# Keys and values on 64-row tiles in two parts, TensorE in groups of four chunks

## The chip, the cores and the metric

The kernel runs on one core of a Trainium2 chip. The metric is the device time of one launch in microseconds. Engines are named as in the profile: PE is TensorE's matmuls, PEld its weight loads, DVE is VectorE, ACT is ScalarE, POOL is GpSimd, SP is SyncE.

## The reference

A gated cross-attention block, followed by a mixture of experts. With LN for a layer norm without gain:

```
q = LN(x) Wq^T + bq            x: (32, 56, 256), 16 heads of 16
k, v = ctx Wk^T + bk, ctx Wv^T + bv      ctx: (32, 1500, 256)
p = softmax(clip(q k^T / 4, -50, 50))    masked keys at -50
d = clip(rs) * ((p v) Wo^T + bo)
x = x + tanh(g_xattn) * (LN(d) * gamma + beta)
router: top 2 of 8 experts on LN(x), softmax of the two logits
x = x + tanh(g_ffn) * sum_e w_e * relu(LN(x) Wfc_e)^2 Wproj_e
```

All is float32. The context has 48,000 rows of 256, so most of the work is keys and values, then scores and P times V.

## The kernel before

Float32 accuracy is reached with fp32r operands in two summands, high and low: a product is three matmuls (high x high, high x low, low x high). This holds for keys, values, scores and experts. P times V is a plain fp32 matmul, which the trace shows as two instructions.

**Tiling.** Batches are taken in pairs (`pair(i)`, 16 of them). The 1500 keys of a batch are 3 groups of 4 chunks of 125 keys, so a pair has 24 chunks (PC) in 6 groups (PG). `pair` runs over u = 0 to 11, two chunks each; q = u // 2 is the group and half = u % 2. While the chunks of group q are used, keys and values of the next group (n = i * PG + q + 1) are made, a half at each u.

**TensorE.** At each u: `scores` of two chunks, `k_proj` of one half (128 of the 256 key features for all 500 keys: 6 matmuls, 128 rows contracted, 500 columns), `v_proj` of one half (two chunks of keys, 12 matmuls, 128 rows contracted, 256 columns), on some u a side step (`spread_sums`, `x_transpose`, `q_proj`, `out_proj`, `y_transpose`, and the router in the last pair), then `pv` of the two chunks before. Scores use 64-row tiles, in pairs on rows 0-63 and 64-127. `pv` has 16 heads a chunk, on column tiles of 32.

**Buffers.** The scores have four banks of PSUM (`sc_ps`), two chunks. `k_ps` has a bank for each half; bank 0 is also the side steps' (`side_ps`). `v_ps` is one bank for both halves, and `o_ps` one. Keys (`kh`, `kl`), values (`vst`) and split context (`c_hi`, `c_lo`) are double in SBUF. The probabilities (`prob`) have PB = 4 buffers of one chunk.

**The other engines,** in an order written out by hand for each u. ScalarE: `ctx_high` (once a group), `exps` of two chunks, `k_hi_evac`, copies of the side steps. VectorE: `before_clips` (side work that depends on u), `ctx_low`, `clip` of two chunks, `k_lo_evac`, `v_evac_step`. GpSimd takes powers and some subtractions. SyncE loads a context group as soon as `ctx_low` has freed its buffer, and does the four `pack` DMAs behind the load of q = 0. Everything is ordered by semaphores: `pv` waits for `clip_done` and `v_evac`, `v_proj` for `v_evac` of the half before, `k_proj` for `k_lo`, `exps` for `scores_done` and for `pv_done` of the chunk PB earlier, `scores` for `exp_done` of the chunk two earlier.

After the attention the experts run over 7 tiles of 256 tokens. The change doesn't touch them but for the P times V that remains at their start.

Of the kernel before, what the change touches and what calls it, by code (L numbers as in the profile page):

```python
# [14 lines left out]
B, S, D, T = 32, 56, 256, 1500  # L15
NH, HD = 16, 16
P = 128
KD = D // P
TC = 125
GC = 4  # L20
# [14 lines left out]
FT = 256  # L35
NF = TOK // FT
VW = HD + 1
PB = 4
UN = PC // 2
NW = 2 * NE  # L40
NB = 4
# [12 lines left out]
def gated_cross_attention_moe(nc, a, x1_dram, out):  # L54
# [5 lines left out]
    with ExitStack() as ctx:  # L60
        def sem(name):
            return ctx.enter_context(nc.semaphore(name))
# [134 lines left out]
        ctx_split = sem("ctx_split")  # L197
        kproj_done = sem("kproj_done")
        vproj_done = sem("vproj_done")
        k_hi = sem("k_hi")  # L200
        k_lo = sem("k_lo")
        v_evac = sem("v_evac")
# [163 lines left out]
        def _(pe):  # L366
# [19 lines left out]
            def v_proj(n, half, s):  # L386
# [8 lines left out]
                                   wv_hi[:, k, :], wv_lo[:, k, :], k == 0, k == KD - 1)  # L395
                last.then_inc(vproj_done, 1)

            def scores(i, c):

                n = i * PC + c  # L400
                b, g = c // NC, c // GC
                if c % NC == 0:
                    pe.wait_ge(q_ready, 4 * i + 2 * b + 2)
                if c % GC == 0:
                    pe.wait_ge(k_lo, KD * (i * PG + g + 1))
                wait(pe, exp_done, n - 1)
                cs = slice(c % GC * TC, (c % GC + 1) * TC)
                for m in range(KD):
                    for term, (k, q) in enumerate(((kh, q_hi), (kh, q_lo), (kl, q_hi))):
                        for r in range(2):  # L410
                            rows = slice(r * HW, (r + 1) * HW)
                            last = pe.matmul(sc_ps[0:TC, 2 * (c % 2) + r, m * HS * S:(m + 1) * HS * S],  # L412
                                             k[rows, g % 2, m, cs], q[rows, b, m, :, :], start=term == 0, stop=term == 2)
                last.then_inc(scores_done, 1)

            def pv(i, c):

                n = i * PC + c
                if c % NC == 0:
                    wait(pe, o_evac, 2 * i + c // NC)  # L420
                if c % 2 == 0:
                    pe.wait_ge(v_evac, i * UN + c // 2 + 1)
# [52 lines left out]
            def pair(i, first=False, final=False):  # L475
                freed = {}
                if not first:
                    freed.update({0: (ylo_done, i), 2: (sum_evac, i), 8: (dlt_evac, i)})
                if not final:
                    freed.update({4: (xT_done, i + 2), 6: (qT_done, i + 2)})  # L480
                for u in range(UN):
                    q, half = divmod(u, 2)
                    n = i * PG + q + 1
                    more = not (final and q == PG - 1)
                    scores(i, 2 * u)
                    if first and u == 0:
                        pe.wait_ge(v_evac, 2)
                    scores(i, 2 * u + 1)
                    if more:
                        k_proj(n, half, (q + 1) % 2, freed.get(u))  # L490
                        v_proj(n, half, (q + 1) % 2)
                        if half == 1:
                            pe.wait_ge(k_lo, KD * n + 1)
                    if u == 1 and not first:
                        spread_sums(i - 1)
                    if u == 3 and not final:
                        x_transpose(i + 1)
                    if u == 5 and not final:
                        q_proj(i + 1)
                    if u == 7 and not first:  # L500
                        out_proj(i - 1)
                    if u == 10 and final:
# [5 lines left out]
                    if u == 11 and not first:  # L508
                        y_transpose(i - 1)
                    if first and u == 1:  # L510
                        pe.wait_ge(o_clear, 1)
                    if not (first and u == 0):
                        for d in (2, 1):
                            pv(*((i, 2 * u - d) if u > 0 else (i - 1, PC - d)))

            pe.wait_ge(cst_in, 16)
            x_transpose(0, first_side)
# [59 lines left out]
            pe.wait_ge(welo_done, NW)  # L577
            pe.wait_ge(exp_done, B * NC - 1)
            fc(0, 0)
            for d in (2, 1):  # L580
                pv(NP - 1, PC - d)
            experts(0, first=True)
            experts(1)
# [7 lines left out]
        def _(act):  # L591
# [65 lines left out]
            def pair(i, first=False, final=False):  # L657
                for u in range(UN):
                    q, half = divmod(u, 2)
                    if u == 0 and not final:  # L660
                        load_xq(i + 1)
                    if u == 10:
                        if not first:
                            store_x1(i - 1)
                        load_xr(i)
                        if not final:
                            load_matrix(i + 1)
                    if half == 0 and not (final and q >= PG - 2):
# [5 lines left out]
                    if u == 1:  # L674
                        if not first:
                            sums_spread(i - 1)
                        expert_hi(i)
                    if u == 3 and not final:
                        x_transposed(i + 1)
                    if u == 11 and not first:  # L680
                        y_transposed(i - 1)
                    if u == 11 and final:
                        second_of_two(0)

# [52 lines left out]
        def _(dve):  # L737
# [179 lines left out]
            def pair(i, first=False, final=False):  # L917
                for u in range(UN):
                    q, half = divmod(u, 2)
                    before_clips(i, u, first, final)  # L920
                    if not (final and q >= PG - 2):
                        ctx_low(i * PG + q + 2, half, q % 2)
                    clip(i, 2 * u)
                    clip(i, 2 * u + 1)
                    if not (final and q == PG - 1):
                        k_lo_evac(i * PG + q + 1, half, (q + 1) % 2)
                        v_evac_step(i * PG + q + 1, half, (q + 1) % 2)
                if not first:
                    y_low(i - 1)

            def before_clips(i, u, first, final):

                if u == 0:
                    q_split(i, 1)
                if u == 1:
                    if not first:
                        o_evac_step(i - 1, 1)
                        sums_split(i - 1, 1)
                    q_high(i, 1)
                if u == 2:  # L940
                    if not final:
# [15 lines left out]
                if u == 6 and not final:  # L957
                    q_evac(i + 1)
                    q_split(i + 1, 0)
                if u == 7:  # L960
                    o_evac_step(i, 0)
                    sums_split(i, 0)
                    if not final:
                        q_high(i + 1, 0)
                if u == 8:
                    if not first:
                        delta(i - 1)
# [168 lines left out]
```

## Time and profile before

| | us |
|---|---|
| median of 3 runs | 1268.37 (1267.36 to 1270.18) |
| profiled execution, its own time | 1267.26 |
| its span | 1265.1 |
| mean granted TensorE clock | 0.997 |
| busy: PE, PEld, DVE, ACT, POOL | 1248.7, 1129.9, 964.8, 688.5, 174.6 |

The span reaches from the first to the last instruction; the time is 2.2 us longer. Matmuls are pipelined: the duration of one (0.28 us, say) is longer than the time to the start of the next, so pitches are read from starts.

### The profile page before, as it was taken

What the parts mean: (1) busy time and instruction counts of PE and PEld (TensorE: products, weight loads), DVE (VectorE), ACT (ScalarE), POOL (GpSimd) and SP (SyncE); (2) the same over time, 40 slices, a digit from 0 to 9 for tenths busy, and PEclk for the clock granted to TensorE, in tenths of its full rate; (3) what the DMA queues carried; (4) which work ended last, traced back from release to release, by engine and by line L of the source; (5) the groups of instructions that cost most, each with busy time, mean ns of one, the idle gap of its engine ahead of it and who ended that gap; (6) DMA issues with size and microseconds to landing.
All of it is one profiled execution on the core that took longest, in us unless ns stands there. A gap on an engine that the chain in (4) does not pass through costs nothing.

```text
span 1265.1 us, 51469 instructions
## 1 busy us (share of the span) xinstructions
PE 1248.7 (99%) x22040; PEld 1129.9 (89%) x22040; DVE 964.8 (76%) x1806; ACT 688.5 (54%) x854; POOL 174.6 (14%) x142
## 2 busy tenths in 40 slices
PE   7999999999999999999999999999999999899998
PEld 6888888888888888888888888888888888899998
DVE  6678777878787877787777878787878777687555
ACT  5555555556555556565555555565555565344443
POOL 1000101010101010010001010101010100154443
PEclk9999999999999999999999999999999999899999
DMA  5121212121112112121211121211121120010000
GB/s 158 52 67 43 64 53 70 53 66 56 55 51 68 55 42 71 47 70 53 70 50 57 53 70 53 67 55 54 51 69 55 45 74 5 19 64 10 17 8 17
DMA packets 29507, 68.19 MB, mean 54 GB/s; under 512 B 6037, under 2 KB 13458, under 8 KB 29330
## 3 DMA queue, kind: packets, MB, share of 16 engines
q1 hardware_dynamic: 20450, 54.61, 14.2%
q10 hardware_dynamic: 8880, 10.75, 2.6%
q8 instruction: 168, 2.75, 0.9%
q14 instruction: 9, 0.07, 0.0%
HBM read 60.77 MB, written 3.67 MB: 51 GB/s over the span
## 4 chain that ended last, share of the span: by engine, by line
PE 94%; issue 2%; DVE 1%; POOL 1%; ACT 0%; DMA 0%; DVEq 0%; POOLq 0%; ACTq 0%
PE sc_ps L412 23%; PE o_ps L427 14%; PE k_ps L369 10%; PE v_ps L370 7%; PE v_ps L369 7%; PE v_ps L371 7%; PE k_ps L371 7%; PE k_ps L370 7%; PE sc_ps L369 3%; PE sc_ps L370 3%; PE sc_ps L371 3%; PE k_ps L444 1%; POOL h_lo L352 1%; PE k_ps L457 1%; DVE h_sq L1043 0%
## 5 line engine op out<-in xcount | busy, mean ns | idle before, releaser
L610 ACT ACTIVATE prob<-sc_ps,m_bias 125x896 f32<-125x896 f32 x384 | 366.3, 1005 | 321.8 <-PE sc_ps L412 321.8
L915 DVE TENSOR_SCALAR prob<-prob 125x896 f32<-125x896 f32 x384 | 245.1, 642 | 140.8 <-ACT prob L610 137.4
L412 PE MATMUL sc_ps<-q_hi,kh 64*125 64x224 f32 x1536 | 228.5, 294 | 0.0
L370 PE MATMUL v_ps<-wv_lo,c_hi 128*125 128x256 f32 x764 | 214.8, 281 | 0.0
L369 PE MATMUL v_ps<-wv_hi,c_hi 128*125 128x256 f32 x764 | 214.3, 280 | 0.0
L371 PE MATMUL v_ps<-wv_hi,c_lo 128*125 128x256 f32 x764 | 214.0, 280 | 0.0
L412 PE MATMUL sc_ps<-q_hi,kl 64*125 64x224 f32 x1536 | 209.8, 270 | 0.0
L412 PE MATMUL sc_ps<-q_lo,kh 64*125 64x224 f32 x1536 | 209.3, 269 | 0.0
L427 PE MATMUL o_ps<-prob,vst 125*17 125x56 f32 x12288 | 189.2, 214 | 0.0
L427 PEld LDWEIGHTS o_ps<-prob,vst 125*17 125x17 f32 x12288 | 158.3, 98 | 31.5 <-issue 9.8
L763 DVE SCALAR_TENSOR_TENSOR kl<-k_ps,cst,kh 128x500 fp32r<-128x500 f32 x192 | 141.5, 738 | 46.5 <-ACT kh L597 44.7
L369 PE MATMUL k_ps<-c_hi,wk_hi 128*128 128x500 f32 x384 | 169.7, 442 | 0.9 <-DVE c_lo L769 0.9
L412 PEld LDWEIGHTS sc_ps<-q_hi,kh 64*125 64x125 f32 x1536 | 144.8, 185 | 17.7 <-issue 0.2
L597 ACT ACTIVATE kh<-k_ps,cst 128x500 fp32r<-128x500 f32 x192 | 130.5, 680 | 43.3 <-PE k_ps L371 41.0
L371 PE MATMUL k_ps<-c_hi,wk_lo 128*128 128x500 f32 x384 | 149.6, 390 | 0.0
L370 PE MATMUL k_ps<-c_lo,wk_hi 128*128 128x500 f32 x384 | 149.3, 389 | 0.0
L370 PEld LDWEIGHTS v_ps<-wv_lo,c_hi 128*125 128x125 f32 x764 | 141.8, 186 | 7.6
L369 PEld LDWEIGHTS v_ps<-wv_hi,c_hi 128*125 128x125 f32 x764 | 141.9, 186 | 7.2
L316 POOL TENSOR_TENSOR rstd<-var_e,mhalf 112x1 f32<-112x1 f32 x48 | 69.2, 1442 | 560.1 <-DVE var_e L753 560.1
L412 PEld LDWEIGHTS sc_ps<-q_hi,kl 64*125 64x125 f32 x1536 | 145.9, 187 | 0.0
L412 PEld LDWEIGHTS sc_ps<-q_lo,kh 64*125 64x125 f32 x1536 | 145.4, 186 | 0.0
L371 PEld LDWEIGHTS v_ps<-wv_hi,c_lo 128*125 128x125 f32 x764 | 141.9, 186 | 0.0
(129 smaller groups left out, 1913.7 us busy)
## 6 DMA issues: line engine op xcount, KB each, us to landing
raw<-in_ctxT SPq DMA_DIRECT2D x96, 500.0 KB, 3.5
w_raw<-in_we ACTq DMA_DIRECT2D x16, 256.0 KB, 3.7
xq<-in_x ACTq DMA_DIRECT2D x16, 112.0 KB, 2.0
xr<-in_x ACTq DMA_DIRECT2D x16, 112.0 KB, 3.6
x_scratch<-x ACTq DMA_DIRECT2D x16, 112.0 KB, 3.7
out_y<-acc SPq DMA_DIRECT2D x7, 256.0 KB, 2.0
acc<-x_scratch SPq DMA_DIRECT2D x1, 1280.0 KB, 6.3
rec<-rec SPq DMA_DIRECT2D x64, 14.0 KB, 2.3
```

The lines of the kernel that those rows point to most:

```text
L316: pool.tensor_tensor(rstd[ln][0:PW, :], var_e[ln][0:PW, :], mhalf[0:PW, :], ALU.pow)\
L352: pool.tensor_tensor(h_lo[:, e % NB, :, :], h_sq[:, e % 2, :, :], plain(h_hi[:, e % NB, :, :]), ALU.subtract).then_inc(hlo_done, 1)
L369: pe.matmul(ps, w_h, m_h, start=first, stop=False)
L370: pe.matmul(ps, w_h, m_l, start=False, stop=False)
L371: return pe.matmul(ps, w_l, m_h, start=False, stop=last)
L412: last = pe.matmul(sc_ps[0:TC, 2 * (c % 2) + r, m * HS * S:(m + 1) * HS * S], k[rows, g % 2, m, cs], q[rows, b, m, :, :], start=term == 0, ...
L427: last = pe.matmul(o_ps[q * 32:q * 32 + VW, col * S:(col + 1) * S], vst[0:TC, c // GC % 2, c % GC, h, :], prob[0:TC, c % PB, at * S:(at + ...
L444: last = pe.matmul(bank[:, m * PW:(m + 1) * PW], wq[:, k, m * P:(m + 1) * P], xnT[:, k, :], start=(k == 0), stop=(k == KD - 1))
L597: act.activation(kh[:, s, m, :], k_ps[:, m, 0:TG], ACT.Identity, bias=bk[:, m:m + 1]).then_inc(k_hi, 1)
L610: act.activation(prob[0:TC, c % PB, :].rearrange("p (c n) -> p c n", c=2), sc_ps[0:TC, 2 * (c % 2):2 * (c % 2) + 2, 0:NH * S // 2], ACT.Ex ...
L763: dve.scalar_tensor_tensor(kl[:, s, m, :], k_ps[:, m, 0:TG], bk[:, m:m + 1], plain(kh[:, s, m, :]), ALU.add, ALU.subtract).then_inc(k_lo, 1)
L915: dve.tensor_scalar(p, p, EXP_LO, EXP_HI, ALU.max, ALU.min).then_inc(clip_done, 1)
```

## The change

- `k_proj` and `v_proj` inside `pair` are replaced by `kv_part`. It contracts over 64 rows at a time, in two parts. For each k and each of the three terms it issues a value matmul (chunk j = 0), a key matmul and a value matmul (j = 1); in part 0 keys use rows 0-63 and values rows 64-127, in part 1 the other way round. The number of matmuls for keys and values doubles, each contracts over half the rows, and columns stay as they were. Part 1 waits for part 0 by two new semaphores. The first group of all is still made by `k_proj` and `v_proj`.
- TensorE's `pair` runs over the 6 groups: `pv` of the four chunks of the group before, then parts and chunks of scores in turn, with the side step between the third part and the fourth chunk.
- `pv` waits for each chunk's own `clip_done`. PB goes from 4 to 6.
- ScalarE and VectorE get another order within u: the half's key and value evacuations come ahead of the second `exps` and `clip` when half = 0, and the value evacuation comes ahead of the keys'. Some side work of `before_clips` moves by one u: `o_evac_step` and `sums_split` of the pair before from u = 1 to 0, those of the first batch from 7 to 6, `q_evac` from 6 to 5, `delta` from 8 to 7; `y_low` moves from the end of the pair to u = 11.

```diff
-PB = 4
+PB = 6
...
+            def kv_terms(s, k):
+
+                return ((wk_hi, c_hi[:, s, k, :]), (wk_hi, c_lo[:, s, k, :]), (wk_lo, c_hi[:, s, k, :])), \
+                       ((c_hi[:, s, k, :], wv_hi), (c_hi[:, s, k, :], wv_lo), (c_lo[:, s, k, :], wv_hi))
+
+            def kv_part(n, half, s, part, side=None):
+
+                if part == 0:
+                    if half == 0:
+                        pe.wait_ge(ctx_split, KD * (n + 1))
+                    if side:
+                        wait(pe, *side)
+                    wait(pe, k_lo, KD * (n - 1) + half + 1)
+                    wait(pe, v_evac, 2 * n + half)
+                else:
+                    pe.wait_ge(kpart_done, 2 * (n - 1) + half + 1)
+                    pe.wait_ge(vpart_done, 2 * (n - 1) + half + 1)
+                k_rows = slice(part * HW, (part + 1) * HW)
+                v_rows = slice((1 - part) * HW, (2 - part) * HW)
+                ws = slice(half * P, (half + 1) * P)
+                for k in range(KD):
+                    k_terms, v_terms = kv_terms(s, k)
+                    for t in range(3):
+                        begin, end = part == 0 and k == 0 and t == 0, part == 1 and k == KD - 1 and t == 2
+                        w, c_m = k_terms[t]
+                        c_s, w_m = v_terms[t]
+                        for j in range(2):
+                            cs = slice((2 * half + j) * TC, (2 * half + j + 1) * TC)
+                            v_last = pe.matmul(v_ps[0:TC, j * D:(j + 1) * D], c_s[v_rows, cs], w_m[v_rows, k, :],
+                                               start=begin and j == 0, stop=end, skip_group_check=True)
+                            if j == 0:
+                                k_last = pe.matmul(k_ps[:, half, 0:TG], w[k_rows, k, ws], c_m[k_rows, :],
+                                                   start=begin, stop=end)
...
@@ TensorE, pv
-                    pe.wait_ge(clip_done, n + 2)
+                pe.wait_ge(clip_done, n + 1)
@@ TensorE, pair
+                for q in range(PG):
                     n = i * PG + q + 1
+                    c, slot = GC * q, (q + 1) % 2
                     more = not (final and q == PG - 1)
...
+                        for d in range(GC, 0, -1):
+                            pv(*((i, c - d) if q > 0 else (i - 1, PC - d)))
+                    if more:
+                        kv_part(n, 0, slot, 0, freed.get(2 * q))
+                    scores(i, c)
+                    if more:
+                        kv_part(n, 0, slot, 1)
...
+                    scores(i, c + 1)
...
+                    scores(i, c + 2)
+                    if more:
+                        kv_part(n, 1, slot, 0)
+                        pe.wait_ge(k_lo, KD * n + 1)
+                    beside_scores(i, q, first, final)
+                    scores(i, c + 3)
+                    if more:
+                        kv_part(n, 1, slot, 1)
@@ ScalarE, ctx_high and pair
+                wait(act, kproj_done, KD * (n - 1))
...
                     exps(i, 2 * u)
-                    exps(i, 2 * u + 1)
-                    if not (final and q == PG - 1):
-                        k_hi_evac(i * PG + q + 1, half, (q + 1) % 2)
...
+                    if half == 1:
+                        exps(i, 2 * u + 1)
+                    if not (final and q == PG - 1):
+                        k_hi_evac(i * PG + q + 1, half, (q + 1) % 2)
+                    if half == 0:
+                        exps(i, 2 * u + 1)
@@ VectorE, pair
                     clip(i, 2 * u)
-                    clip(i, 2 * u + 1)
+                    if u == 11 and not first:
+                        y_low(i - 1)
+                    if half == 1:
+                        clip(i, 2 * u + 1)
                     if not (final and q == PG - 1):
+                        v_evac_step(i * PG + q + 1, half, (q + 1) % 2)
                         k_lo_evac(i * PG + q + 1, half, (q + 1) % 2)
-                        v_evac_step(i * PG + q + 1, half, (q + 1) % 2)
...
+                    if half == 0:
+                        clip(i, 2 * u + 1)
```

## Rows read from the trace of the kernel before

**Rows 1.** The page: busy us of the engines, and the chain that ended last.

```profile
PE 1248.7 (99%) x22040; PEld 1129.9 (89%) x22040; DVE 964.8 (76%) x1806; ACT 688.5 (54%) x854; POOL 174.6 (14%) x142
...
PE 94%; issue 2%; DVE 1%; POOL 1%; ACT 0%; DMA 0%; DVEq 0%; POOLq 0%; ACTq 0%
```

**Rows 2.** Busy time of the attention: stretch, then PE, PEld, DVE, ACT, POOL, clock, DMA.

```profile
22.00:1095.00 1073.00, 1073.00 (x20613) 957.07 (x20612) 839.59 (x1557) 611.29 (x728) 98.53 (x76) 1.00 0.18 56
```

**Rows 3.** Timeline of PE: start, us, engine, line, operation, out<-in, shapes, count.

```profile
507.51 0.38 PE L427 MATMUL o_ps<-prob,vst 125*17 125x56 f32 x16
507.82 0.37 PE L412 MATMUL sc_ps<-q_hi,kh 64*125 64x224 f32 x2
508.03 0.27 PE L412 MATMUL sc_ps<-q_lo,kh 64*125 64x224 f32 x2
...
509.12 0.28 PE L412 MATMUL sc_ps<-q_hi,kl 64*125 64x224 f32 x2
509.32 0.49 PE L369 MATMUL k_ps<-c_hi,wk_hi 128*128 128x500 f32 x1
509.66 0.39 PE L370 MATMUL k_ps<-c_lo,wk_hi 128*128 128x500 f32 x1
...
510.78 0.28 PE L369 MATMUL v_ps<-wv_hi,c_hi 128*125 128x256 f32 x1
...
512.08 0.28 PE L371 MATMUL v_ps<-wv_hi,c_lo 128*125 128x256 f32 x1
512.29 0.98 PE L427 MATMUL o_ps<-prob,vst 125*17 125x56 f32 x64
513.20 0.37 PE L412 MATMUL sc_ps<-q_hi,kh 64*125 64x224 f32 x2
```

**Rows 4.** Timeline of PE: a transpose, and the P times V behind it.

```profile
506.62 0.36 PE L436 MATMUL k_ps<-cst,xn 112*128 112x112 f32 x2
506.91 0.98 PE L427 MATMUL o_ps<-prob,vst 125*17 125x56 f32 x64
```

**Rows 5.** Timeline of PE, two matmuls of the router.

```profile
1079.97 0.26 PE L472 MATMUL k_ps<-wr,yT_hi 128*128 128x16 f32 x1
1080.08 0.26 PE L469 MATMUL k_ps<-wr,yT_hi 128*128 128x16 f32 x1
```

**Rows 6.** Timeline of ACT and DVE: exp, clip and value evacuation.

```profile
508.87 1.91 ACT L610 ACTIVATE prob<-sc_ps,m_bias 125x896 f32<-125x896 f32 x2 [0.57 <-PE sc_ps L412]
...
509.91 0.63 DVE L915 TENSOR_SCALAR prob<-prob 125x896 f32<-125x896 f32 x1 [0.30 <-ACT prob L610]
...
512.49 0.69 DVE L778 TENSOR_TENSOR vst<-v_ps,rowv 125x512 f32<-125x512 f32 x1
```

**Rows 7.** Timeline of DVE at u = 9, the side work and what follows.

```profile
536.39 0.40 DVE L757 TENSOR_SCALAR dlt<-dlt,mv,rstd 112x256 f32<-112x256 f32 x1
...
538.60 0.67 DVE L769 TENSOR_TENSOR c_lo<-raw,c_hi 128x500 fp32r<-128x500 f32 x1
539.18 1.16 DVE L915 TENSOR_SCALAR prob<-prob 125x896 f32<-125x896 f32 x2
```

**Rows 8.** Timeline: the one key matmul that waits for VectorE.

```profile
18.64 0.67 DVE L769 TENSOR_TENSOR c_lo<-raw,c_hi 128x500 fp32r<-128x500 f32 x1
...
19.37 0.49 PE L369 MATMUL k_ps<-c_hi,wk_hi 128*128 128x500 f32 x1 [0.86 <-DVE c_lo L769]
```

**Rows 9.** Timeline of DVE at u = 2, first side work and next c_lo.

```profile
496.33 0.42 DVE L748 BATCH_NORM_STATS2 st<-xq 112x6 f32<-112x256 f32 x1
...
498.37 1.00 DVE L769 TENSOR_TENSOR c_lo<-raw,c_hi 128x500 fp32r<-128x500 f32 x1
```

**Rows 10.** Timeline of DVE: the normalised queries' input.

```profile
502.16 0.40 DVE L757 TENSOR_SCALAR xn<-xq,mv,rstd 112x256 f32<-112x256 f32 x1
```

**Rows 11.** Timeline of the SP queue, and the DMAs' time to landing.

```profile
514.92 2.52 SPq L280 DMA_DIRECT2D rec<-rec  x4
...
DMA to landing us min/median/max: 2.3/2.7/3.0
```

More of the change, by code:

```diff
@@ L199, in gated_cross_attention_moe @@
         vproj_done = sem("vproj_done")
+        kpart_done = sem("kpart_done")
+        vpart_done = sem("vpart_done")
         k_hi = sem("k_hi")
@@ L396, in v_proj @@
                 last.then_inc(vproj_done, 1)
+            def kv_terms(s, k):
[28 more added lines that the diff above has]
+                                                   start=begin, stop=end)
+                if part == 0:
+                    k_last.then_inc(kpart_done, 1)
+                    v_last.then_inc(vpart_done, 1)
+                else:
+                    k_last.then_inc(kproj_done, 1)
+                    v_last.then_inc(vproj_done, 1)
             def scores(i, c):
@@ L480, in pair @@
                     freed.update({4: (xT_done, i + 2), 6: (qT_done, i + 2)})
-                for u in range(UN):
-                    q, half = divmod(u, 2)
+                for q in range(PG):
                     n = i * PG + q + 1
+                    c, slot = GC * q, (q + 1) % 2
                     more = not (final and q == PG - 1)
-                    scores(i, 2 * u)
-                    if first and u == 0:
-                        pe.wait_ge(v_evac, 2)
[L488 to L502, printed above, removed]
+                    if first and q == 1:
+                        pe.wait_ge(o_clear, 1)
+                    if not (first and q == 0):
+                        for d in range(GC, 0, -1):
[5 more added lines that the diff above has]
+                        kv_part(n, 0, slot, 1)
+                    if first and q == 0:
+                        pe.wait_ge(v_evac, 2)
+                    scores(i, c + 1)
+                    if not more:
                         pe.wait_ge(ylo_done, NP - 1)
@@ L507, in pair, with beside_scores @@
                             router(0, t)
[L508 to L514, printed above, removed]
+                    scores(i, c + 2)
[6 more added lines that the diff above has]
+                        kv_part(n, 1, slot, 1)
+            def beside_scores(i, q, first, final):
+                if q == 0 and not first:
+                    spread_sums(i - 1)
+                if q == 1 and not final:
+                    x_transpose(i + 1)
+                if q == 2 and not final:
+                    q_proj(i + 1)
+                if q == 3 and not first:
+                    out_proj(i - 1)
+                if q == 5 and not first:
+                    y_transpose(i - 1)
             pe.wait_ge(cst_in, 16)
@@ L579, in _ @@
             fc(0, 0)
-            for d in (2, 1):
+            for d in range(GC, 0, -1):
                 pv(NP - 1, PC - d)
@@ L670, in pair @@
                     exps(i, 2 * u)
-                    exps(i, 2 * u + 1)
-                    if not (final and q == PG - 1):
-                        k_hi_evac(i * PG + q + 1, half, (q + 1) % 2)
[L674 to L677, printed above, removed]
+                    if u == 1 and not first:
+                        sums_spread(i - 1)
                     if u == 3 and not final:
@@ L681, in pair @@
                         y_transposed(i - 1)
+                    if half == 1:
[4 more added lines that the diff above has]
+                        exps(i, 2 * u + 1)
+                    if u == 1:
+                        expert_hi(i)
                     if u == 11 and final:
@@ L923, in pair @@
                     clip(i, 2 * u)
-                    clip(i, 2 * u + 1)
+                    if u == 11 and not first:
+                        y_low(i - 1)
+                    if half == 1:
+                        clip(i, 2 * u + 1)
                     if not (final and q == PG - 1):
+                        v_evac_step(i * PG + q + 1, half, (q + 1) % 2)
                         k_lo_evac(i * PG + q + 1, half, (q + 1) % 2)
-                        v_evac_step(i * PG + q + 1, half, (q + 1) % 2)
-                if not first:
-                    y_low(i - 1)
+                    if half == 0:
+                        clip(i, 2 * u + 1)
             def before_clips(i, u, first, final):
                 if u == 0:
-                    q_split(i, 1)
-                if u == 1:
                     if not first:
@@ L938, in before_clips @@
                         sums_split(i - 1, 1)
+                    q_split(i, 1)
+                if u == 1:
                     q_high(i, 1)
@@ L956, in before_clips @@
                     divide(i - 1)
-                if u == 6 and not final:
+                if u == 5 and not final:
                     q_evac(i + 1)
-                    q_split(i + 1, 0)
-                if u == 7:
+                if u == 6:
                     o_evac_step(i, 0)
                     sums_split(i, 0)
-                    if not final:
-                        q_high(i + 1, 0)
+                if u == 6 and not final:
+                    q_split(i + 1, 0)
+                if u == 7 and not first:
+                    delta(i - 1)
+                if u == 7 and not final:
+                    q_high(i + 1, 0)
                 if u == 8:
                     if not first:
-                        delta(i - 1)
                         delta_statistics(i - 1)
```

## The prediction

> **What bounds the kernel now.** I read the page first. TensorE is busy for 99% of the span, and the chain that ended last runs through TensorE for 94% of it [rows 1]; the reader is to see that the time is the sum of TensorE's instructions. Then the stretches: between 22 and 1095 us TensorE has no idle time at all, at full granted clock, and VectorE is busy 840 of 1073 us, ScalarE 611 [rows 2]. So in the attention no wait is to be won; what counts is the pitch at which matmuls follow each other and what lies between groups. Then TensorE's timeline of one step of two chunks, 5.38 us from first score to first score [rows 3].
>
> In that step (starts, rounded to 10 ns):
> - Scores: pairs on rows 0-63 and 64-127, ten pitches from 508.03 to 509.12, 0.109 us a pair. Twelve pairs make 1.31.
> - Keys: 128 rows, 500 columns, 509.66 to 510.78 is five pitches of 0.224; six make 1.34.
> - Values: 128 rows, 256 columns, 510.78 to 512.08 is eleven pitches of 0.118; twelve make 1.42.
> - P times V: from the 1st to the 49th of 64 is 506.91 to 507.51, 0.0125 each [rows 3, 4]; 64 make 0.80.
>
> The pitches sum to 4.87. The other 0.51 us is paid where the tile shape changes: leaving P·V 0.11 (507.51 + 16 x 0.0125 = 507.71, scores at 507.82); the first score pair takes 0.21 for 0.109, +0.10; score to keys 0.20 for 0.109, +0.09; first key matmul 0.34 for 0.224, +0.11; last value to P·V 0.21 for 0.118, +0.09.
>
> **The change on TensorE.** Per context group of four chunks it now pays 2 x 5.38 = 10.76 us. After: P·V of four chunks in one run, 128 x 0.0125 = 1.60, leaving it 0.11, the first loads bare once, 0.10; scores 24 x 0.109 = 2.62; entering P·V 0.09. All between is on 64-row tiles, with no change of shape. The waits on the half results (kpart_done, vpart_done) cost nothing: at least one chunk of scores, 0.65 us, lies between the parts, against some 0.40 from a matmul's start to a reader's (below). Without that cover each is 0.3 or so.
>
> The new term is a (k, t) step in kv_part: value matmul of 256 columns, key of 500, value of 256. Keys use one half of the rows, values the other. There are 24 steps a group. No row shows unlike matmuls side by side. Bounds: if the value half follows its own pitch, 2 x 0.118 = 0.236; if only the longer single stream counts, the key pitch, 0.224; if each of the two in a half pays what a score matmul pays over its columns (0.109 for 224, where 256 columns of the value row without its 12 ns are 0.107, so 224 are 0.093, leaving 0.016), 2 x 0.123 = 0.245. I take 0.236: score pairs are, as I read them, set by weight loads and not by streaming. The router's matmuls, of 8 or 16 columns, follow each other at 0.11 [rows 5], which can only be the load of 128 columns; the scores' 0.109 is such a load. A value matmul of 0.118 covers one, and a step covers two in turn. So 24 x 0.236 = 5.66, against 2 x (1.34 + 1.42) = 5.52 before.
>
> Sum: 1.60 + 0.11 + 0.10 + 2.62 + 0.09 + 5.66 = 10.18, so -0.58 a group; 95 groups have such a step: **-55 us**.
>
> **Side steps.** The sum spread, the transposes, the query and output projections stood behind the values, in the same 128-row shape: the two matmuls of a transpose then cost 0.29, 506.62 to 506.91 [rows 4], and the change of shape behind them was due anyway. Now they stand between kv_part and scores. Each pays the way into 128 rows, 0.09 + 0.11, and the way back, 0.10 (between the 0.09 and 0.11 of the other changes) + 0.10: 0.40. There are 2 + 14 x 5 + 3 = 75: **+30 us**. If both bare loads were hidden it would be 15.
>
> **The other engines.** Put t = 0 at the start of a group's P·V. kv_part 0 starts at 1.7, first scores at 3.2 with their last pair at 3.76, second part 3.9 to 5.3, two chunks of scores to 6.6, kv_part of half 1 at 6.60, side step and fourth chunk from 8.02, last part to 10.09, next P·V at 10.18.
> - *Value buffer, half 0.* There is one v_ps, so half 1 at 6.60 waits for v_evac. Last score pair to exp is 0.40 (508.03 + 4 x 0.109 = 508.47, exp 508.87), exp to clip 1.04, clip to the next VectorE start 0.53, the evacuation 0.69 [rows 6, 7], VectorE to TensorE 0.06 (19.31 to 19.37, [rows 8]): 3.76 + 2.72 = 6.48. Slack 0.12, nothing paid. Every 0.1 beyond it is 9.5 us.
> - *Front work.* Clip of the first chunk can start at 5.20. VectorE is through with the last group at about t = 1.8 and has then its side work and c_lo. The largest is u = 2, 496.33 to 498.37, 2.04, plus 0.58 [rows 9]: 4.4. Free. At u = 0 o_evac waits for P·V's end at 1.6 + 0.3; with 1.6 of work and c_lo it is 4.1. Free.
> - *xn (u = 3).* The second chunk's clip is from 7.28, xn is out at 7.88 + 0.40 + 0.06 = 8.34 [rows 10]; x_transpose could start at 8.02. The wait of 0.32 hides the 0.10 of the change of shape: +0.22 x 15 = **+3 us**.
> - *u = 9.* x_after and its statistics take 2.21 (536.39 to 538.60, [rows 7]). From 7.84: clips at 10.63 and 11.16, v_evac from 11.76 to 12.45, known at 12.51. The next kv_part is due at 11.87; part of this is felt first at the last chunk's P·V, which waits for clip_done. In all 0.64 x 14 = **+9 us**. Side work up to about 1.55 in that place is free: u = 1 (0.54), u = 3 (about 1.1), u = 7 and 5 (behind the TensorE result that they now wait for, at about 9.3, but their groups are 1.3 longer).
> - *Moved past queues.* q_evac stands ahead of c_lo at u = 5, so SyncE's load and the four packs behind it start some 1.5 us later. The packs take 2.5 to issue and 3 at most to land [rows 11]; from about t = 11 they are in by 17, out_proj is due at 19.5. On ScalarE the side copies moved ahead of the second exp wait for a TensorE step 0.4 earlier, and exp of chunk four comes only after that step anyway.
> - *Nothing.* Six prob buffers: exp of a chunk waits for P·V six earlier, done at the group's start. The further wait of ctx_high lies behind k_hi_evac, which has the same kproj_done. The P·V run at the start of the experts is the same work.
>
> Sum: -55 + 30 + 3 + 9 = -13 on the profiled execution's 1267.3 us (span 1265.1), so 1254.3; the median of the runs, 1268.4, lies 1.1 above it. I say **1255 us**.
>
> **Rivals.**
> 1. *The loads don't overlap* (8%). The change doubles the loads of keys and values: 36 a half where there were 18, each as long as before. If three loads of a step came in turn, a step is 3 x 0.109 = 0.327, +0.091 x 24 x 95 = +207: 1462 us. It decides from a step of 0.242 up, 5.6 ns over mine. Against it: the two loads of a score pair fit in 0.109, and one alone takes 0.11 [rows 3, 5]. For it: those are equal and adjacent, and here a value load must start the moment its predecessor's matmul does.
>  The Trainium skill, "TensorE: Matmul & The Clock Gate", section "LDWEIGHTS (loading the stationary operand)", says that a load's time follows its columns and that fewer rows don't shorten it, (columns over 1.2, in ns). The router's rows agree. By that rule alone halving the rows speeds up nothing and 36 loads a half cost 3.9 us where they are not beside each other; the sum would be rival 1's.
> 2. *Each half pays more per matmul* (17%), step 0.243 to 0.250, most plainly 0.245: +20 to my sum, 1275 us. Slower than before.
> 3. *The chain to v_evac is late* (12%). ScalarE to VectorE to TensorE has 0.12 slack by my count, from rounded rows. With 0.1 to 0.25 missing a group, +10 to +24: 1265 to 1279. For: VectorE's load rises from 78% to some 79%. Against: the idle time ahead of exp, 0.57 in [rows 6], shows ScalarE free.
> 4. *The step takes the key's pitch* (11%), 0.224: -27, 1228 us; the slack of rival 3 shrinks to 0.05, still there.
> 5. *The side steps pay more or less*, 0.2 or 0.6 each: 1240 to 1270; inside the forecast's case.
>
> **Numbers.** Forecast's case, 1238 to 1266: 50%. Rival 1: 8, 2: 17, 3: 12, 4: 11; 2% for anything else. Range 1230 to 1277: it leaves out rival 1, and an edge of 2, 3 and 4. 0.2%, 2.5 us, is about what a measurement of this kernel can tell from no change. Faster by more: 50 + 11, and 4 of rival 3: 65%. Same: 7% (between rivals 2, 3 and the case's upper end). Slower: 28%. By the case alone the range is 1240 to 1265.
>
> **What would show it.** A (k, t) step of kv_part: 0.236, with two value matmuls 0.118 apart and the key beside the first. Twenty-four score pairs and 24 steps in sequence with no gap at the borders. Group without side step 10.18. Side steps with 0.20 ahead and 0.20 behind. TensorE waits: on xn once a pair, 0.3; on prob or vst at u = 9, 0.6; on vst in the middle of a group none. I am wrong if the step is beyond 0.242, if that last wait is there in each group, or if the borders between scores and parts cost as a change of shape does.

## The result, and the profile after

The changed kernel takes 1259.16 us, median of 4 runs (1258.86 to 1261.05), against 1267.86 before: ratio 0.9931, interval 0.9914 to 0.9948. That is 8.7 us less. The forecast was 1255 against 1268.4, 13 less. The profiled execution has its own time of 1259.26 us and a span of 1257.2.

The page after; engines, instruction queue (packets, MB, share of the DMA engines) and chain, beside [rows 1]:

```profile
PE 1235.6 (98%) x25460; PEld 1175.5 (94%) x25460; DVE 920.3 (73%) x1806; ACT 697.3 (55%) x854; POOL 171.1 (14%) x142
...
q8 instruction: 196, 3.21, 1.0%
...
PE 94%; issue 2%; DVE 2%; POOL 1%; DMA 0%; ACT 0%; DVEq 0%; POOLq 0%
```

TensorE has 3420 matmuls and as many loads more, and is busy 13 us less. Its attention is no longer free of idle time (as [rows 2]):

```profile
22.00:1085.00 1063.00, 1058.12 (x23924) 1000.38 (x23922) 794.20 (x1555) 622.07 (x729) 95.18 (x76) 0.99 0.19 57
```

The timeline of PE in a group without a side step, from its P times V on, to be held against [rows 3]:

```profile
526.33 1.77 PE L469 MATMUL o_ps<-prob,vst 125*17 125x56 f32 x128
528.03 0.38 PE L428 MATMUL v_ps<-wv_hi,c_hi 64*125 64x256 f32 x1
528.03 0.49 PE L431 MATMUL k_ps<-c_hi,wk_hi 64*128 64x500 f32 x1
...
528.37 0.38 PE L431 MATMUL k_ps<-c_lo,wk_hi 64*128 64x500 f32 x1
528.37 0.39 PE L428 MATMUL v_ps<-wv_lo,c_hi 64*125 64x256 f32 x2
528.59 0.38 PE L431 MATMUL k_ps<-c_hi,wk_lo 64*128 64x500 f32 x1
528.60 0.40 PE L428 MATMUL v_ps<-wv_hi,c_lo 64*125 64x256 f32 x2
...
529.31 0.39 PE L428 MATMUL v_ps<-wv_hi,c_lo 64*125 64x256 f32 x2
529.50 0.31 PE L454 MATMUL sc_ps<-q_hi,kh 64*125 64x224 f32 x2
```

The step is as forecast: after the first, four value steps lie between 528.37 and 529.31, 0.235 each, with the key beside them. The key's own pitch is 0.22 (528.37, 528.59), so it runs ahead of the values. At the border to the scores nothing is paid: 529.31 to 529.50 is 0.19, less than a step. This P times V starts at 526.33 and the next at 536.53, a group of 10.20; I had 10.18.

A group with a side step, the query projection, 64 rows to 128 and back:

```profile
511.19 0.40 PE L428 MATMUL v_ps<-wv_hi,c_lo 64*125 64x256 f32 x2
511.52 1.15 PE L486 MATMUL k_ps<-xnT,wq 128*128 128x112 f32 x8
512.60 0.37 PE L454 MATMUL sc_ps<-q_hi,kh 64*125 64x224 f32 x2
512.80 0.27 PE L454 MATMUL sc_ps<-q_lo,kh 64*125 64x224 f32 x2
```

The way in takes 0.33 where a value step takes 0.235, the first load lies inside the eight, and the first score pair takes 0.20 for 0.109. From the starts of P times V, groups with the query projection take 11.48, so 1.28 over a bare one; before, that side step added 0.88. That is +0.40, the term of the forecast. Taken the same way, by medians over pairs 2 to 13, the sum spread costs 0.47 more than before, the transpose of x 0.50, the output projection 0.38.

VectorE at u = 9, and the P times V that waits for its clips (compare [rows 7]):

```profile
534.09 0.41 DVE L813 TENSOR_SCALAR dlt<-dlt,mv,rstd 112x256 f32<-112x256 f32 x1
...
536.30 0.67 DVE L825 TENSOR_TENSOR c_lo<-raw,c_hi 128x500 fp32r<-128x500 f32 x1
536.88 1.16 DVE L971 TENSOR_SCALAR prob<-prob 125x896 f32<-125x896 f32 x2
537.95 0.68 DVE L834 TENSOR_TENSOR vst<-v_ps,rowv 125x512 f32<-125x512 f32 x1
```

```profile
536.53 2.36 PE L469 MATMUL o_ps<-prob,vst 125*17 125x56 f32 x128
538.82 0.38 PE L428 MATMUL v_ps<-wv_hi,c_hi 64*125 64x256 f32 x1
```

That run lasts 2.36 us, others 1.77: 0.59 in this pair. In most pairs the run loses 0.39, and some 0.17 more stands between it and the next value matmul: the group takes 11.3 us, and 10.77 in the variant without the delay (below), so 0.55, where 0.64 was forecast. The view of waits shows it hardly at all: most of it is cut into pieces inside a run of pipelined matmuls.

The middle pairs, from the first score of pair 2 to that of pair 14, in the kernel before and then in the changed one:

```profile
149.85 0.37 PE L412 MATMUL sc_ps<-q_hi,kh 64*125 64x224 f32 x2
955.85 0.37 PE L412 MATMUL sc_ps<-q_hi,kh 64*125 64x224 f32 x2
```

```profile
151.78 0.30 PE L454 MATMUL sc_ps<-q_hi,kh 64*125 64x224 f32 x2
950.56 0.30 PE L454 MATMUL sc_ps<-q_hi,kh 64*125 64x224 f32 x2
```

That is 67.17 a pair before and 66.57 after. So -0.60 a pair; my terms made -0.62 (6 x -0.58, 5 x 0.40, 0.22, 0.64). Fourteen such pairs give -8.4, nearly all of what was measured (8.7 between the medians, 7.9 between the two profiled spans). The 4 us that the forecast had on top should have come from the first and the last pair. What took them is in two views. At the start, TensorE's waits and clock:

```profile
PE v_ps L428 <- DVE c_lo L825: 2.6, 1, 2.6
```

```profile
16.00:26.00 10.00, 7.45 (x82) 7.24 (x82) 6.45 (x18) 3.14 (x4) 0.00 (x0) 0.83 0.18 53
...
1065.00:1100.00 35.00, 32.56 (x481) 30.93 (x479) 22.77 (x55) 11.20 (x18) 5.26 (x4) 0.80 0.06 18
```

The first kv_part now stands ahead of the first scores, so the wait for c_lo, 0.86 before [rows 8], has nothing in front of it; the granted clock in that stretch is 0.83, before it was 1.00. At the end the same 35 us have 0.80; before it was 0.90:

```profile
1065.00:1100.00 35.00, 32.28 (x608) 29.53 (x607) 20.65 (x53) 11.17 (x16) 2.78 (x3) 0.90 0.06 16
```

Between the levels of 2.4 and 1.2 GHz that is 14 us at the lower one for 7, so 3.5 us of work lost, if all of it is paid. In both kernels the clock falls in the midst of the router's matmuls of 8 and 16 columns. These are views of one execution each: over the whole span the clock was 0.993 in all four runs of the changed kernel and between 0.994 and 0.997 in those of the kernel before.

### The profile page after: what moved, and what is told of

It is laid out like the page before. It is cut to its first block, busy times and chain, and to the rows that moved or that the text cites. A ratio compares the mean times of both kernels' runs of the same rounds, so it can differ in the third digit from the quotient of the medians.

```text
span 1257.2 us, 58770 instructions
## 1 busy us (share of the span) xinstructions
PE 1235.6 (98%) x25460; PEld 1175.5 (94%) x25460; DVE 920.3 (73%) x1806; ACT 697.3 (55%) x854; POOL 171.1 (14%) x142
## 4 chain that ended last, share of the span: by engine, by line
PE 94%; issue 2%; DVE 2%; POOL 1%; DMA 0%; ACT 0%; DVEq 0%; POOLq 0%
PE v_ps L428 24%; PE k_ps L431 21%; PE sc_ps L454 21%; PE o_ps L469 12%; PE sc_ps L371 3%; PE sc_ps L372 3%; PE sc_ps L373 3%; PE k_ps L499 1%; PE k_ps L486 1%; POOL h_lo L354 1%; DVE prob L971 1%; PE k_ps L493 1%; PE k_ps L478 0%; PE k_ps L505 0%; DMA xq<-in_x 0%
## 5 line engine op out<-in xcount | busy, mean ns | idle before, releaser
L428 PE MATMUL v_ps<-wv_hi,c_hi 64*125 64x256 f32 x1520 | 317.3, 288 | 3.7 <-DVE c_lo L825 2.6
L431 PE MATMUL k_ps<-c_hi,wk_hi 64*128 64x500 f32 x760 | 314.1, 413 | 0.0
L428 PE MATMUL v_ps<-wv_hi,c_lo 64*125 64x256 f32 x1520 | 301.1, 277 | 0.0
L428 PE MATMUL v_ps<-wv_lo,c_hi 64*125 64x256 f32 x1520 | 300.9, 278 | 0.0
L431 PE MATMUL k_ps<-c_lo,wk_hi 64*128 64x500 f32 x760 | 293.2, 386 | 0.0
L431 PE MATMUL k_ps<-c_hi,wk_lo 64*128 64x500 f32 x760 | 292.2, 384 | 0.0
L428 PEld LDWEIGHTS v_ps<-wv_hi,c_hi 64*125 64x125 f32 x1520 | 225.4, 183 | 16.9 <-DVE c_lo L825 2.8
L428 PEld LDWEIGHTS v_ps<-wv_hi,c_lo 64*125 64x125 f32 x1520 | 229.4, 183 | 0.0
L428 PEld LDWEIGHTS v_ps<-wv_lo,c_hi 64*125 64x125 f32 x1520 | 228.4, 183 | 0.0
L431 PEld LDWEIGHTS k_ps<-c_lo,wk_hi 64*128 64x128 f32 x760 | 141.6, 186 | 0.0
```

The lines of the kernel that those rows point to most:

```text
L428: v_last = pe.matmul(v_ps[0:TC, j * D:(j + 1) * D], c_s[v_rows, cs], w_m[v_rows, k, :], start=begin and j == 0, stop=end, skip_group_check ...
L431: k_last = pe.matmul(k_ps[:, half, 0:TG], w[k_rows, k, ws], c_m[k_rows, :], start=begin, stop=end)
```

## The experiments

**P times V merged, keys and values left on 128 rows.** In the kernel before:

```diff
-PB = 4
+PB = 6
-                        for d in (2, 1):
-                            pv(*((i, 2 * u - d) if u > 0 else (i - 1, PC - d)))
+                    if half == 0 and not (first and q == 0):
+                        for d in range(GC, 0, -1):
+                            pv(*((i, GC * q - d) if q > 0 else (i - 1, PC - d)))
                     scores(i, 2 * u)
```

> The kernel before with the P times V of four chunks in one run at the start of a group (and six buffers, one clip wait a chunk), keys and values still on 128 rows. My theory (the gain is the number of changes of tile shape): one entry and one exit of P times V fewer a group, 0.09 + 0.11 + 0.10, against one more key-to-score border, 0.19: about -0.11 to -0.14 us in each of 96 groups, side steps at their old cost, so 1255 to 1258 us, as fast as the changed kernel. Rival (the gain comes from keys and values on 64-row tiles): no more than 2 us faster than before.

Measured: 1272.7 us (11 runs), ratio 1.003, interval 1.0019 to 1.0040. The theory missed: it is 4 us slower. The rival's bound (no more than 2 us faster) holds, but not for its reason. A bare group takes 10.64 for 10.76, so the 0.12 was there, and of the 0.56 by which the changed kernel's bare group is shorter 0.44 comes with the 64-row parts and their order. But TensorE now stands still at places where no engine is waited for. Its waits from 100 to 1050 us, where before it had none:

```profile
PE sc_ps L412 <- issue: 4.8, 8, 2.4
PE k_ps L371 <- issue: 2.5, 1, 2.5
PE o_ps L427 <- issue: 1.5, 2, 1.2
PE v_ps L371 <- issue: 1.3, 1, 1.3
```

From the starts, 15 gaps of over 0.2 us make 13.7 us there. They fall in scores, keys or values as well as in P times V. All end 2.3 to 3.0 us after the start of a transfer of the instruction queue. Those transfers are 16 KB. In this kernel there are 168 and TensorE has 2 x 22040 instructions, after the change 196 and 2 x 25460: 28 transfers more for 6840 instructions more, some 250 each. Counted from one transfer to the next in the attention, TensorE starts 255 to 257 instructions on average, in both kernels. So the queue feeds TensorE, a block of 256 instructions at a time. New theory: a run of P times V over four chunks is 256 instructions in 1.6 us, a whole block, and where a block is used up before its successor has come, TensorE stands still.

**Scores first in the very first group.**

```diff
+                    early = first and q == 0
+                    if early:
+                        scores(i, c)
+                        pe.wait_ge(v_evac, 2)
+                        scores(i, c + 1)
                     if more:
                         kv_part(n, 0, slot, 0, freed.get(2 * q))
```

> The changed kernel, but in the very first group the two chunks of scores come ahead of the first half, as before. Theory: TensorE's wait of 2.6 us on c_lo goes, and the stretch at half clock after it: 3 to 4.5 us faster than the changed kernel (1259.2), so 1255 to 1256. Rival (start-up is set by VectorE and DMA anyway): within 1 us of 1259.2.

Measured: 1258.05 us, ratio 0.9912 (0.9897 to 0.9928). The wait falls from 2.6 to 0.9 and the clock from 16 to 26 us is 1.00 again, but only about 1 us comes out, and that is inside the intervals. The trace shows where the rest went. The first score of pair 2 comes at 149.80 and not at 151.78, 2.0 us earlier; at pair 14 it is 949.75 for 950.56, so 1.2 of the 2.0 are lost between. The gaps over 0.2 us from 100 to 1050 us sum to 8.7 here and to 6.7 in the changed kernel (those of u = 9, mostly 0.35, in both).

**The second statistics out of u = 9.**

```diff
                     x_after(i - 1)
-                    x_after_statistics(i - 1)
                 if u == 10 and not first:
-                    normalised(2, i - 1, dlt, x1).then_inc(y_done, 1)
+                    x_after_statistics(i - 1)
...
                         k_lo_evac(i * PG + q + 1, half, (q + 1) % 2)
+                    if u == 10 and not first:
+                        normalised(2, i - 1, dlt, x1).then_inc(y_done, 1)
```

> The changed kernel, with the second statistics of u = 9 moved to u = 10 and the normalised y behind the evacuations of u = 10. Theory: P times V at the group after u = 9 falls from 2.26 to 1.70 us, no new wait elsewhere: 14 x 0.57 = 8 us faster than 1259.2, so 1251. Rival (the delay moves on to y_transpose or to the value buffer's wait in group 5): under 3 us faster.

Measured: 1257.10 us, ratio 0.9906 (0.9890 to 0.9922): 2 us of 8, and the interval overlaps the changed kernel's. The mechanism is right: the run at that place takes 1.77 like any other in most pairs, and its group 10.77. The gain is gone elsewhere, and not in the rival's waits. TensorE's waits now show more of the nameless kind ("issue", no engine waited for) at P times V, 1.3 us in three before:

```profile
PE o_ps L469 <- issue: 3.8, 8, 0.8
```

From the starts, 6.7 us of gaps over 0.15 stand in P times V of this kernel's attention with no late clip ahead of them. My reading, which no run tests by itself: while VectorE held TensorE up, the instructions had time to come.

**Keys thinned, values thinned.** Matmuls of two of three terms are left out, keys in the one, values in the other; one execution of each.

```diff
-                            if j == 0:
+                            if j == 0 and t == 0:
                                 k_last = pe.matmul(k_ps[:, half, 0:TG], w[k_rows, k, ws], c_m[k_rows, :],
```

> The changed kernel with the key matmuls of two of the three terms left out (so the keys are less exact); four of six steps of a part hold value matmuls alone. Theory (a step is the value half's own pitch, the key matmul is free): a part stays at 1.41 us and the time within 3 us of 1259. Rival (both halves share a cost): a bare step falls below 0.23, the time by over 10 us.

> The changed kernel with the value matmuls of two of the three terms left out (so the values are less exact). Theory (a step is the larger of the value half's 2 x 0.118 and the key half's 0.224): the steps without values follow at 0.225, so a part is 2 x 0.236 + 4 x 0.225 = 1.37 and a group 4 x 0.045 less: 95 x 0.18 = 17 us less, 1242, less what waits appear. Rival (each of two matmuls side by side pays something for the other): steps of 0.21 or less, 1230 or below.

Measured: 1259.36 us with the keys thinned, the time of the changed kernel; 1247.52 with the values thinned. PE's timeline of the second, a part, in which the second, third, fifth and last of the six keys (from 524.39, 524.62, 525.07 and 525.30) have no values of their own:

```profile
524.39 0.39 PE L433 MATMUL k_ps<-c_lo,wk_hi 64*128 64x500 f32 x1
524.40 0.40 PE L429 MATMUL v_ps<-wv_hi,c_hi 64*125 64x256 f32 x2
524.62 0.39 PE L433 MATMUL k_ps<-c_hi,wk_lo 64*128 64x500 f32 x1
524.85 0.38 PE L433 MATMUL k_ps<-c_hi,wk_hi 64*128 64x500 f32 x1
524.86 0.36 PE L456 MATMUL sc_ps<-q_hi,kh 64*125 64x224 f32 x1
525.07 0.39 PE L433 MATMUL k_ps<-c_lo,wk_hi 64*128 64x500 f32 x1
525.08 0.36 PE L456 MATMUL sc_ps<-q_lo,kh 64*125 64x224 f32 x1
525.30 0.39 PE L433 MATMUL k_ps<-c_hi,wk_lo 64*128 64x500 f32 x1
```

Keys follow at 0.225, the pitch of the 128-row form [rows 3]. So the step is the longer of two independent halves and neither pays for the other; with the keys thinned the values keep their 0.235. That the time stays is in part chance: the bare group falls from 10.20 to 9.95, where scores start early on the rows that the keys leave free, and new waits take it back (7.0 us without a named releaser in the attention for 1.3, 7.1 on prob and vst for 0.2). A bare group falls to 9.89, not 10.02, since the value half doesn't wait for the keys: it has the second pair of values at 524.40, beside the second key, and by these records takes score matmuls that stand behind the keys in the program. The time stays 5 us above the 1242 forecast all the same: groups with a side step fall by 0.08 to 0.21 only, and the waits in the attention sum to 12.2 us on prob, vst and without a named releaser, for 1.5 in the changed kernel.

**Side steps next to P times V.** The core of the edit (ScalarE's copies, `q_evac`, `delta` and `y_low` go back behind them):

```diff
-                        pe.wait_ge(k_lo, KD * n + 1)
-                    beside_scores(i, q, first, final)
                     scores(i, c + 3)
                     if more:
                         kv_part(n, 1, slot, 1)
+                        pe.wait_ge(k_lo, KD * n + 1)
+                    beside_scores(i, q, first, final)
```

> The changed kernel with the side step behind the group's last part, next to P times V, as before the change, and the copies that wait for it put later to fit. Theory (a side step inside the 64-row run pays a way back, 0.10 + 0.10, that it need not pay): 0.20 x 75 = 15 us less, plus 1 to 2 for the wait on xn, so 1242 to 1245 us. Rival 1 (P times V then starts when VectorE has had longer, but instructions are fetched too late): gaps at P times V give back 3 to 8: 1247 to 1252. Rival 2 (the side bank is free too late for the next group's first part): waits of some 0.3 in five of six groups, no gain.

Measured: 1252.78 us, ratio 0.9870 (0.9853 to 0.9887), just above rival 1's range. The group with the query projection takes 11.27 for 11.48, -0.21, as forecast. The gaps grow, in the waits 9.4 us at P times V in 14 cases, and from the starts 18 us over 0.2 in all, some 4.5 of them the late clips of u = 9.

**All three edits together.**

> The changed kernel with all three edits: scores first in the very first group, side steps next to P times V, the second statistics of u = 9 moved to u = 10. Theory: as for the side steps alone, a further 1 for the start and 8 for u = 9, so 1234 to 1237. Rival (late instructions at P times V): the edits save 24 and the gaps cost 6 to 12, so 1240 to 1247.

Measured: 1244.48 us, ratio 0.9811 (0.9798 to 0.9824), within the rival's range. This trace shows the gaps alone. From 100 to 690 us there is none in the view of waits; from 690 to 1030 us:

```profile
PE o_ps L469 <- issue: 11.9, 12, 1.6
```

One of them, in the timeline of PE:

```profile
931.93 1.60 PE L469 MATMUL o_ps<-prob,vst 125*17 125x56 f32 x113
935.10 0.39 PE L469 MATMUL o_ps<-prob,vst 125*17 125x56 f32 x15 [1.57 <-issue]
935.42 0.38 PE L428 MATMUL v_ps<-wv_hi,c_hi 64*125 64x256 f32 x1
```

A run is broken off after 113 of 128 instructions. The last instruction transfer starts at 932.81, 0.5 us before the last matmul of the first piece; the run goes on 2.3 us after its start. In the 2 us ahead of that start other DMAs keep the 16 DMA engines 85% busy (DMA share, last figure but one):

```profile
930.80:932.80 2.00, 2.00 (x86) 1.72 (x85) 1.36 (x3) 1.53 (x3) 0.00 (x0) 1.00 0.85 240
```

**Half of P times V.** The kernel of u = 9 with heads 8 to 15 left out, so half of the attention is missing (`o_ps` is preset to 1 in place of 0):

```diff
-                for h in range(NH):
+                for h in range(NH // 2):
```

> The variant of u = 9 with heads 8 to 15 left out of P times V (so half of the output's attention is missing). The run at the start of a group is then 128 instructions in 0.8 us, not 256 in 1.6. Theory (the gaps at P times V are instructions that come too late because a run uses them too fast): the irregular gaps, 6.7 us in the attention of that variant, fall to under 1; time about 1257 - 96 x 0.80 - 6 = 1174. Rival (the gaps are late clips or something of the data): they stay at 5 or more, 1180.

Measured: 1202.76 us, one execution. The gaps are gone as forecast: P times V has none over 0.2 us left. The time is 29 us above the forecast, for another reason, which these rows of its timeline show:

```profile
500.56 0.98 PE L469 MATMUL o_ps<-prob,vst 125*17 125x56 f32 x64
501.83 0.35 PE L428 MATMUL v_ps<-wv_hi,c_hi 64*125 64x256 f32 x1 [0.28 <-DVE vst L834]
```

With the run halved, the value buffer is what TensorE waits for, 0.28 in each group (21.9 us in 88 waits). These waits also give the instructions time, so the run doesn't separate a shorter burst from a slower group. The slack of 0.5 us that P times V gives there was smaller than the 0.8 taken away.

**Four buffers.** `PB = 4` in the changed kernel.

> The changed kernel with four probability buffers in place of six. Theory (all four chunks' P times V is done at the start of a group, 1.6 us in, and the first exp comes at 4.2): nothing, within 1.5 us of 1259.2. Rival (exp of a group then waits for P times V): ScalarE waits on TensorE's o_ps, 2 us or more slower.

Measured: 1259.91 us, ratio 0.9937 (0.9923 to 0.9950). Within the 1.5 us of the forecast.

**The same instructions, shifted.** Small matmuls ahead of the first transpose, where TensorE waits for its input:

```diff
             pe.wait_ge(cst_in, 16)
+            for _ in range(32):      # 8, 16 in the other two
+                pe.matmul(first_side[0:32, 0:32], ident[:, 0:32], ident[:, 0:32], start=True, stop=True)
             x_transpose(0, first_side)
```

> The kernel with all three edits, and 32 small fp32 matmuls (64 with their second pass, 128 instructions with the loads) ahead of the first transpose, where TensorE waits anyway. It shifts everything that follows by half a block of 256 instructions. Theory (a gap at P times V comes where a block of 16 KB is used up in the run before the next has come): the gaps, which were all after 697 us, lie elsewhere, above all in the first half; their sum changes too, and with it the time, by up to 15 us either way, less than 1 us being the shift's own cost. Rival (gaps come from something in the data or the DMA load late in the run): they stay where they were, after 697 us, 14 to 17 us in sum.

> As the padded kernel, with 8 small matmuls (32 instructions) in place of 32. With no padding the gaps began at 697 us; with 128 instructions the quiet stretch lies behind about 830 us, some 10 pairs later, so 128 instructions are about 10 pairs and 32 about 2.5. Theory (position in the block of 256 instructions decides): the quiet stretch ends some 2.5 pairs later, at about 860 us, and if none comes in at the front 5 to 10 us are saved on 1244.5: 1235 to 1240. Rival (the gaps depend on time or on how far the run is): first gap at 700 again, 1244.

> As the padded kernel, with 16 small matmuls (64 instructions). Theory (position in the block decides): the quiet stretch ends some 5 pairs later, after 1000 us; gaps at the front if it is shorter than 14 pairs, in the first 100 to 300 us. Time 1235 to 1250, by how many these are. Rival (time or data): first gap at 700 again, 1244.

| instructions ahead | us, median | ratio to before (interval) | gaps over 0.2 us, 100 to 1050 us | where |
|---|---|---|---|---|
| 0 | 1244.48 | 0.9811 (0.9798 to 0.9824) | 15.5 | all after 696 |
| 32 | 1232.86 | 0.9732 (0.9714 to 0.9750) | 3.1 | two early, the rest from 1000 on |
| 64 | 1240.75 | 0.9789 (0.9775 to 0.9802) | 6.2 | 109 to 538 |
| 128 | 1264.62 | 0.9968 (0.9958 to 0.9979) | 24.6 | 110 to 1017 |

The stretch from 20 to 100 us, which the table leaves out, adds 0.8, 0.9, 4.6 and 6.3 us, from the first row to the last.

The waits of the one with 128 ahead, from 100 to 690 us, where with none ahead there were none:

```profile
PE sc_ps L454 <- issue: 7.4, 11, 2.0
PE v_ps L428 <- issue: 4.8, 9, 1.5
PE k_ps L431 <- issue: 0.6, 2, 0.4
PE o_ps L469 <- issue: 0.5, 1, 0.5
```

The work that follows is the same in all four, and the times differ by 32 us. The rival (something in the data, or a load late in the run) falls, since the gaps don't stay after 697 us. Of the expectations, 32 instructions did better than its range (1235 to 1240), with the quiet stretch 4 to 5 pairs longer, not 2.5; 64 is inside its range, but its gaps run on to 538 and not only to 300; 128 costs 20 us and not at most 15. So the position in the block decides when gaps come; how long a quiet stretch is I could not derive, only shift.

One rival is still open. The context loads stand at a fixed place in each group, so instructions put ahead shift the instruction transfers against these loads too, not only against the runs of P times V. The traces point that way. I counted transfers from 100 to 1050 us in whose last 2 us before the start the DMA engines were over half busy. With 128 ahead, 22 of the 25 transfers behind a gap over 0.4 us were such, and 41 of the 146 others; with P times V merged on 128 rows, 11 of 12 and 30 of 132; with all three edits and none ahead, 6 of 12 and 31 of 161. But in the variant of u = 9 it was none of 7. So a transfer that comes late behind other DMAs seems to be part of many gaps and isn't needed for one; no run moves the loads alone.

## Why the prediction was right, point by point

- **Pitches and changes of shape.** Right: a bare group is 10.20 for 10.18. The step of 0.236 was taken from the value half's own pitch, and rows and both thinned kernels bear that out. The Trainium skill ("TensorE: Matmul & The Clock Gate", "LDWEIGHTS (loading the stationary operand)") says that a load isn't shortened by fewer rows, and the traces agree: a value load takes 186 ns on 128 rows before and 183 on 64 after. But 36 loads a half don't lengthen a step beyond 0.235, since the loads of the two row halves overlap; rival 1 is refuted by the trace, and rivals 2 and 4 with it.
- **Side steps, 0.40 each.** Right: +0.40 at the query projection, and half of it comes back when the step stands next to P times V (-0.21). The others lie between 0.35 and 0.50. By the forecast's terms it is the dearest thing in the change: 30 us of the 55 gained.
- **u = 9.** Right in place and nearly in size, 0.55 for 0.64. What I hadn't seen is that its removal gives only 2 us.
- **xn.** Too high. The transpose of x costs 0.50 more than before and not 0.62, so the wait is 0.1.
- **The value buffer, half 0.** Right: none of the changed kernel's waits stands there. Rival 3 argued with a VectorE share that rises from 78% to 79%; it fell to 75% (794 of 1063 us). The half P times V kernel shows how near the next one, at the group's start, is.
- **Six buffers at nothing.** Right, and four would do.
- **The first and the last pair.** Where the sum failed: it took 95 groups at -0.58 as if the ends were like the middle, 4 us of the 13. Instead the first part waits 2.6 us for c_lo, and the granted clock is lower at both ends. With the scores first (above), pair 2 starts 2.0 us earlier, so the start accounts for about half of the 4 us, though only 1 of it reaches the time. The end was not tested: its share is read from the clock rows alone.
- **Instructions as a resource.** Missing from the forecast. In the changed kernel itself it takes little, some 2 us of irregular gaps; in the variants with all three edits it took 3 to 25 us and decided what they were worth. That so little of it fell on the changed kernel is luck as far as the runs show: with all three edits the same code, shifted by 128 instructions, took 20 us more.

The version with all three edits and 32 instructions ahead beats both kernels: 1232.86 us, 2.7% under the kernel before. Its time depends on the exact number of instructions ahead of the loop.

## What to carry to other kernels

When one engine is the bound and never waits, count its changes of tile shape: here each was 0.1 to 0.2 us, and putting unlike work on one shape paid even with twice the number of matmuls. But a small step of the old shape left in the middle of the new run pays both ways; put it beside another change that is due anyway. And before merging short instructions into a long run, look at how many instructions a microsecond it uses: a nameless wait ("issue") that moves when code ahead of it is lengthened, and ends some 2 to 3 us after an instruction transfer starts, points to late instruction supply.

## What the runs showed of the hardware that wasn't expected

- TensorE's instructions come in blocks of 16 KB, about 256, and nearly every gap over 0.4 us ends 2.2 to 3.1 us after the start of such a transfer. With runs of 256 instructions in 1.6 us in the program, gaps of up to 2.7 us appear, and 32 to 128 instructions put ahead of the same code change the time by up to 32 us in 1240. How much of that is the position in the block and how much the meeting with other DMAs is open.
- Matmuls on the two halves of the rows go on independently in these traces: keys at 0.225 beside pairs of value matmuls at 0.235, the key stream creeping ahead, and, by the records of the thinned kernels, score matmuls of a free half starting before keys that stand earlier in the program (524.86 and 525.07). A bare group of 9.89 us, where steps in turn would make 10.02, agrees with the records.
- Value matmuls of 256 columns on 64 rows keep the 0.118 pitch that they had on 128.
